# A state-space scan cut into two spans of chunks, with the router of the mixture inside the second span

## The chip, the cores and the metric

The kernel runs on one core of a Trainium2 chip. The metric is the time of one execution on the device, in microseconds, lower is better. The time before is 2651.47 us, the median of three runs (2647.59 to 2654.21). The profile is of one execution on the same core, with a span of 2646.7 us.

The program drives five engines, each with its own list of instructions: TensorE (PE in the rows; its weight loads are PEld), VectorE (DVE), ScalarE (ACT), GpSimd (POOL) and SyncE (SP, which only issues DMAs here).

## The reference, cut to what matters

Two layers work on 4096 tokens (two sequences of 2048) of width 256. The first layer (attention and a fused mixture, up to about 1607 us in the profile) is not touched. The second has a state-space block and a mixture of 20 experts of which each token takes two, each followed by a residual and a layer norm:

```python
# state-space block: u is (2, 2048, 256), 16 states per channel
A = -jnp.exp(log_A)
dt = jax.nn.softplus(u @ W_dt.T + b_dt + dt_bias)
Bt = (u @ W_B.T + b_B).reshape(b, l, d, n)
Ct = (u @ W_C.T + b_C).reshape(b, l, d, n)
A_bar = jnp.exp(dt[..., None] * A)
x_in = (A_bar - 1.0) / A * Bt * u[..., None]
# h = A_bar * h + x_in along the tokens; y = sum over n of Ct * h; y + D_skip * u
x = _layernorm(x + y)

# mixture of experts: E = 20, K = 2
h = gelu(xf @ wg1 + bg1)
probs = softmax((h @ wg2 + bg2)[:, :E])
top_vals, top_idx = top_k(probs, 2)
y = sum over the two chosen experts of top_val * (xf @ We[e] + be[e])
x = _layernorm(x + y)
```

## The kernel before

The tokens are cut into 8 chunks of 512 (CH); a chunk is 4 tiles of 128 tokens. The 256 channels are two halves (KT) of 128 partitions.

**The scan** (`phase_scan`, L1618). The work is 256 units: for each of the 16 states n, for each half m of the channels, for each of the 8 chunks. TensorE (L1681 to L1703) makes B and C of the unit, each from six products in fp32r (high and low parts of weights and tokens, L1684 to L1686), into rings of four and two PSUM banks. ScalarE makes the decay exp(dt A) (`decay`, L1724) and copies C with its scale (`outward`, L1732). VectorE makes (B + b) u (`driven`, L1838), times (decay - 1) (`decayed`, L1845), and the recurrence over 512 tokens (`scan`, L1853, instruction L1858). GpSimd multiplies the states by C (`multiply`, L1791, instruction L1797) and adds them to y (L1812). Each pair (n, m) needs its own weights; they are loaded raw, copied by ScalarE into the high part, and VectorE takes the low part from the two (`round_w`, L1826, instruction L1831), once for 8 units. The low parts of the tokens are made at the start (`round_lo`, L1833, instruction L1835, and L1816 on GpSimd). The states of n = 1 to 14 are a loop in each engine's program.

**The mixture** (`phase_mixture`, L1958) is a block of its own that begins when all engines have left the scan. First, for each chunk, comes what is called gating below. `turn_z` (L2133) turns y by 8 transposes, ScalarE copies it, VectorE takes mean and variance (`means`, L2406) and normalises (`normalise`, L2416). `turn_x` (L2143) turns it back by 8 transposes, `hide` (L2151) is the hidden layer, ScalarE applies gelu, `logits` (L2162) gives the 20 scores. The tiles form three groups of 8, 12 and 12 (chunks 0 and 1; 2 to 4; 5 to 7). For each group VectorE takes softmax and the two largest (`choose`, L2429), TensorE counts how many tokens chose each expert (`count`, L2172), VectorE turns the counts into a place for each token in a list sorted by expert (`settle`, L2454, and `list_tiles`, L2473), and GpSimd writes the tokens' rows to their places in DRAM by indirect DMAs (`scatter`, L2103, instruction L2108: 16, 24 and 24 of them).

Then 62 pairs of list tiles (18, 22 and 22 for the groups) go through the experts: SP loads a pair's 256 rows (`load`, L2075), TensorE turns them (`turn_rows`, L2184, instruction L2191), ScalarE copies them, TensorE multiplies them by the expert's weights and adds the bias (`experts`, L2194, instructions L2202 and L2203), ScalarE (first 18 pairs) or VectorE copies the answer, and SP stores it. The gating of chunks 5 to 7 lies among the first pairs (`hide(5)` at pair 3, `count(2)` at pair 14, `exponent(2)` on ScalarE at pair 11). GpSimd gathers the answers back by 64 indirect DMAs (`gather`, L2111, instruction L2119), those of the last group only when all pairs are stored; VectorE combines (`combine`, L2487) and normalises (`finish`, L2504), and ScalarE's queue stores the output.

## Time and profile before

| | |
|---|---|
| median of three runs | 2651.47 us |
| the profiled execution: its span | 2646.7 us |
| TensorE busy | 93% of the span |
| VectorE, ScalarE, GpSimd busy | 74%, 52%, 42% |
| mean granted TensorE clock | 0.972 |
| first matmul of the scan | 1610.0 us |
| end of the scan on TensorE | about 2340.2 us |
| first expert product | 2415.0 us |
| last expert product | about 2601.2 us |

The profiled execution has no time of its own beside its span; the difference of 4.8 us to the median is the part outside the first and the last instruction, and the spread of the runs. All positions are from the span's start. A row of stretches names for each engine its busy time in the stretch and in brackets how many instructions; matmuls are pipelined, so that two of them overlap in the rows and a mean duration is longer than the time from one start to the next.

### The profile page before, as it was taken

The numbers are of one execution on the slowest core, as the hardware profiler recorded it, in microseconds if no ns is written. First come the engines' busy times: TensorE is split into PE (matmuls) and PEld (weight loads), VectorE is DVE, ScalarE is ACT, GpSimd is POOL, SyncE is SP. The second block draws the span as 40 slices with busy tenths as digits, with TensorE's granted clock in tenths as the row PEclk, the third lists the DMA queues.
The fourth block names the chain that finished last, engine by engine and source line by source line (L and its number), as shares of the span: only waits on it lengthen the run. The fifth ranks groups of instructions, "written<-read, shape, count | busy, mean of one in ns | idle before, by whom it ended". The sixth has DMA issues, their size and how long they took to land. (4 is left out here: it accounts for less than half of the span.)

```text
span 2646.7 us, 43896 instructions
## 1 busy us (share of the span) xinstructions
PE 2472.2 (93%) x15059; PEld 1552.6 (59%) x15059; DVE 1964.7 (74%) x4037; ACT 1382.1 (52%) x2469; POOL 1110.7 (42%) x1092
## 2 busy tenths in 40 slices
PE   7999999999999999899999997999999999977992
PEld 4433333333333333467777775888888888855772
DVE  3777777777777774266676657999999999975256
ACT  3466666666666666444455535655555555543320
POOL 3522222222222221110000004999989898944454
PEclk9999999999999999999999998999999999987996
DMA  8633333323333321100000000000000000024785
GB/s 244 174 70 71 82 58 58 58 58 58 58 58 69 70 64 66 54 16 17 16 24 25 9 17 8 13 12 12 12 12 12 12 12 12 4 86 130 238 282 162
DMA packets 109601, 166.41 MB, mean 63 GB/s; under 512 B 15876, under 2 KB 74296, under 8 KB 106232
## 3 DMA queue, kind: packets, MB, share of 16 engines
q1 hardware_dynamic: 99064, 143.24, 21.5%
q0 software_dynamic: 6144, 16.79, 2.0%
q10 hardware_dynamic: 4224, 4.19, 0.5%
q8 instruction: 99, 1.62, 0.3%
q14 instruction: 70, 0.57, 0.1%
HBM read 97.66 MB, written 62.01 MB: 60 GB/s over the span
## 5 line engine op out<-in xcount | busy, mean ns | idle before, releaser
L644 ACT ACTIVATE ssm_in_dt<-att_s 128x512 f32<-128x512 f32 (+3 forms) x1280 | 610.0, 535 | 346.9 <-PE att_s L541 182.7
L733 DVE TENSOR_REDUCE att_partmax<-att_s 128x1 f32<-128x512 f32 x768 | 494.3, 686 | 109.8 <-PE att_s L515 66.4
L541 PE MATMUL att_s<-att_qs,att_ks 49*128 49x512 f32 (+3 forms) x1280 | 433.9, 419 | 16.1 <-ACT ssm_in_dt L644 13.8
L515 PE MATMUL att_s<-att_ks,att_qs 49*128 49x512 f32 (+3 forms) x1280 | 434.5, 424 | 4.9 <-DVE att_qs L723 4.7
L541 PEld LDWEIGHTS att_s<-att_qs,att_ks 49*128 49x128 f32 x1280 | 207.4, 185 | 380.3 <-ACT ssm_in_dt L644 307.6
L1797 POOL TENSOR_TENSOR ssm_cc<-ssm_cc,ssm_h 128x512 f32<-128x512 f32 x256 | 334.9, 1308 | 75.7 <-DVE ssm_h L1858 73.8
L432 POOL TENSOR_SCALAR_AFFINE_SELECT ssm_in_dt<-ssm_in_dt 128x256 f32<-128x256 f32 x256 | 104.6, 409 | 621.5 <-ACT ssm_in_dt L644 562.8
L584 PE MATMUL att_o_ps<-ssm_in_dt,att_vst 128*32 128x512 f32 (+3 forms) x2560 | 340.6, 542 | 5.3 <-ACT ssm_in_dt L644 5.3
L1812 POOL TENSOR_TENSOR ssm_out_z<-ssm_out_z,ssm_cc 128x512 f32<-128x512 f32 x256 | 340.4, 1330 | 0.1
L1737 ACT ACTIVATE ssm_cc<-ssm_c_ps,ssm_cur 128x512 f32<-128x512 f32 x256 | 199.0, 777 | 211.8 <-PE ssm_c_ps L1686 211.5
L736 DVE CUSTOM_DVE_ANT_0 att_hid<-att_s,att_hidden 128x512 bf16<-128x512 f32 (+3 forms) x512 | 238.8, 487 | 94.6 <-PE att_s L515 93.7
L1858 DVE TENSOR_TENSOR_SCAN ssm_h<-ssm_a_ps,ssm_h,ssm_inp 128x512 f32<-128x512 f32 x192 | 243.8, 1270 | 0.1
L1730 ACT ACTIVATE ssm_a_ps<-ssm_in_dt,ssm_cur 128x512 f32<-128x512 f32 x256 | 176.4, 689 | 114.5 <-DVE ssm_h L1858 108.5
L515 PEld LDWEIGHTS att_s<-att_ks,att_qs 49*128 49x128 f32 x1280 | 203.9, 185 | 28.1 <-DVE att_partmax L733 10.8
L1842 DVE SCALAR_TENSOR_TENSOR ssm_inp<-ssm_b_ps,ssm_cur,ssm_in_u 128x512 f32<-128x512 f32 x256 | 190.0, 742 | 34.5 <-PE ssm_b_ps L1686 32.7
L1684 PE MATMUL ssm_b_ps<-ssm_hi,ssm_w_hi 128*128 128x512 f32 x512 | 203.5, 398 | 12.7 <-DVE ssm_lo L1835 11.2
L1684 PE MATMUL ssm_c_ps<-ssm_hi,ssm_w_hi 128*128 128x512 f32 x512 | 203.2, 397 | 0.0
L1685 PE MATMUL ssm_c_ps<-ssm_lo,ssm_w_hi 128*128 128x512 f32 x512 | 203.2, 397 | 0.0
L1686 PE MATMUL ssm_c_ps<-ssm_hi,ssm_w_lo 128*128 128x512 f32 x512 | 202.9, 396 | 0.0
L1686 PE MATMUL ssm_b_ps<-ssm_hi,ssm_w_lo 128*128 128x512 f32 x512 | 202.8, 396 | 0.0
L1685 PE MATMUL ssm_b_ps<-ssm_lo,ssm_w_hi 128*128 128x512 f32 x512 | 202.4, 395 | 0.0
L1850 DVE SCALAR_TENSOR_TENSOR ssm_inp<-ssm_a_ps,ssm_inp 128x512 f32<-128x512 f32 x256 | 169.2, 661 | 0.0
(324 smaller groups left out, 4183.7 us busy)
## 6 DMA issues: line engine op xcount, KB each, us to landing
qk_halves<-ssm_in_dt SPq DMA_DIRECT2D x64, 256.0 KB
moe_sorted<-att_hidden SPq DMA_DIRECT2D x31, 512.0 KB, 9.4
moe_rows<-moe_sorted SPq DMA_DIRECT2D x62, 256.0 KB
moe_answers<-moe_mixed SPq DMA_DIRECT2D x62, 256.0 KB
att_far<-bias_tables SPq DMA_DIRECT2D x96, 136.0 KB, 8.5
att_stage_q<-qk_halves SPq DMA_DIRECT2D x96, 128.0 KB, 4.4
att_stage_k<-qk_halves SPq DMA_DIRECT2D x96, 128.0 KB, 5.9
ssm_raw<-in_w_bc SPq DMA_DIRECT2D x30, 256.0 KB, 2.6
```

What stands on the lines that cost most here:

```text
L515: mm = nc.tensor.matmul(s1[:, S1_BANK[at], 0:hi - lo], qs[p % 3][half(b, ROWS), I * P:(I + 1) * P], ks[p % 3][half(b, ROWS), lo:hi], start ...
L541: mm = nc.tensor.matmul(s2[:, turn % RING, 0:hi - lo], ks[p % 3][half(b, ROWS), J * P:(J + 1) * P], qs[p % 3][half(b, ROWS), lo:hi], start ...
L584: mm = nc.tensor.matmul(o_ps[32 * g:32 * g + 32, b, lo:CH], vst[p % 2][b][:, J, :], prob[:, b, step % 2, x * CH + lo:(x + 1) * CH], start= ...
L644: nc.scalar.activation(prob[:, b, step % 2, x * CH + lo:(x + 1) * CH], s2[:, turn % RING, 0:CH - lo], ACT.Exp, scale=1.0 / HD).then_inc(s2 ...
L733: nc.vector.tensor_reduce(most, piece, AX, ALU.max).then_inc(s1_read, 1)
L736: nc.vector.tensor_tensor_reduce(out=hid[HID[at]][:, 0:width], in0=piece, in1=hidden[:, CH - width:CH], scale=1.0, scalar=-3.0e38, op0=ALU ...
L1684: nc.tensor.matmul(out, w_hi, hi[:, k, tok], start=first, stop=False)
L1685: nc.tensor.matmul(out, w_hi, lo[:, k, tok], start=False, stop=False)
L1686: return nc.tensor.matmul(out, w_lo, hi[:, k, tok], start=False, stop=last)
L1797: nc.gpsimd.tensor_tensor(at, at, h[:, i % H_RING], ALU.mult).then_inc(multiplied, 1)
L1812: nc.gpsimd.tensor_tensor(part, part, cc[:, i % Y_RING], ALU.add).then_inc(y_added, 1)
L1858: nc.vector.tensor_tensor_scan(h[:, i % H_RING], a_ps[:, i % A_RING], inp[:, i % 2], 0.0 if first else h[:, (i - 1) % H_RING, CH - 1:CH], ...
```

## The change

The scan and the mixture become one block with one list of instructions for each engine, written out without loops.

- The 256 units are gone through in two parts: first chunks 0 to 4 for all 32 pairs (n, m) (160 units), then chunks 5 to 7 (96 units). The last state of chunk 4 of each pair is kept (`keep_state`) and begins chunk 5. The low and high weights of each pair are stored to DRAM in the first part (512 KB each) and loaded again in the second (`store_halves`, `load_halves`).
- Between the units of the second part stands the gating of chunks 0 to 4, the choices of groups 0 and 1, and the 16 scatters of group 0, at fixed units (`gate(c)` is 161 + 7c). The expert weights are loaded there too, over the parts of u and dt that are no longer read. The 24 scatters of group 1 follow on GpSimd directly behind the last unit.
- The gating of chunks 5 to 7 stands among the pairs, with `turn_z` too (`gate_pair(c)` is 3(c - 5)); `count(2)` moves from pair 14 to 18, `exponent(2)` from 11 to 17. ScalarE copies the answers of 20 pairs instead of 18.
- B has two PSUM banks instead of four, the decay three instead of two; one bank (`spare`) serves all steps of the gating. `round_w` reads the raw weights from this bank, where ScalarE copies them, instead of from SBUF.
- y lies in two segments of 256 tokens for each chunk, so that its transposition can be written over it; GpSimd's addition writes two segments.
- On chunks 0 to 4 ScalarE normalises, and copies both halves of the turned rows.
- A pair's list tiles are interleaved: partition p takes rows 2p and 2p + 1 of the pair (2 KB in one piece) where it took rows p and p + 128 (twice 1 KB). The places that the scatters and gathers use follow it (five small VectorE instructions more for each group).

The diff's core, in the order SyncE, TensorE (units, then pairs), GpSimd, VectorE. `turn_z(c, s)` waits until GpSimd has done the addition of the chunk's last unit (`y_added`).

```diff
-        A_RING, B_RING, C_RING = 2, 4, 2
-        H_RING, Y_RING = 4, 8
+        A_RING, B_RING, C_RING, H_RING, Y_RING = 3, 2, 2, 4, 8
+PART_CHUNKS = ((0, 1, 2, 3, 4), (5, 6, 7))
+HELD = len(PART_CHUNKS[0])
+SPLIT = BLOCKS * HELD
+def gate(turn):
+    return SPLIT + 1 + 7 * turn
+def gate_pair(c):
+    return 3 * (c - HELD)
...
+            def load_halves(b):
+                if b < KT:
+                    eng.wait_ge(halves_stored[b], 16 * N)
+                    eng.wait_ge(c_ready, SPLIT - (KT - 1 - b) * HELD)
+                else:
+                    eng.wait_ge(c_ready, first_unit(b - 1, 1))
+                eng.dma_start(halves[b % KT][:].rearrange("p a k c -> p (a k c)").bitcast(F32), t.halves_bc[b]).then_inc(halves_loaded[b % KT], 16)
...
-                eng.dma_start(rows[p % ROWS][:], t.rows[h][2 * n * P:2 * (n + 1) * P, :].rearrange("(j p) d -> p j d", p=P)).then_inc(rows_loaded[p % ROWS], 16)
+                eng.dma_start(rows[p % ROWS], t.rows[h][2 * n * P:2 * (n + 1) * P, :].rearrange("(p j) d -> p j d", j=2)).then_inc(rows_loaded[p % ROWS], 16)
...
+            for g in range(UNITS):
+                states(g)
+                for c in range(HELD):
+                    for s in range(2):
+                        if g == gate(c) + s:
+                            turn_z(c, s)
+                    for k in range(KT):
+                        if g == gate(c + 2) + 2 + k:
+                            turn_x(c, k)
+                    if g == gate(c + 2) + 4:
+                        hide(c)
+                    if g == gate(c + 3) + 6:
+                        logits(c)
+                if g == gate(6) + 5:
+                    count(0)
+                if g == gate(9) + 5:
+                    count(1)
             turn_rows(0)
             turn_rows(1)
...
             for p in range(PAIRS_ALL):
+                for c in range(HELD, NCH):
+                    for s in range(2):
+                        if p == gate_pair(c) + s:
+                            turn_z(c, s)
+                    if p == gate_pair(c) + 5:
+                        turn_x(c, 0)
+                        turn_x(c, 1)
+                    if p == gate_pair(c) + 6:
+                        hide(c)
+                    if p == gate_pair(c) + 8:
+                        logits(c)
-                if p == 14:
+                if p == 18:
                     count(2)
...
+            for g in range(UNITS):
+                if g + 1 < UNITS:
+                    multiply(g + 1)
+                add(g)
+                for n in range(GROUP_TILES[0]):
+                    for k in range(2):
+                        if g == gate(7) + 3 + 4 * n + 2 * k:
+                            scatter(0, n, k)
+            for n in range(GROUP_TILES[1]):
+                for k in range(2):
+                    scatter(1, n, k)
...
+            for g in range(UNITS):
+                scan(g)
+                if g + 1 < UNITS:
+                    decayed(g + 1)
...
+                if g + 2 < UNITS:
+                    driven(g + 2)
...
+                if g == gate(8) + 2:
+                    share(1)
+                for q in range(3):
+                    if g == gate(8) + 3 + q:
+                        largest(1, q)
+                    if g == gate(8) + 6 + q:
+                        whose(1, q)
+                if g == gate(9) + 2:
+                    chosen(1)
+                if g == gate(9) + 3:
+                    joined(1)
+                if g == gate(9) + 4:
+                    spots(1)
+                if g == gate(9) + 5:
+                    places(1)
```

## Rows read from the trace of the kernel before

**Rows 1.** Busy time by stretch: scan's start, scan, gating, pairs, tail.
```profile
core 0: us, PE busy (x) PEld busy (x) DVE busy (x) ACT busy (x) POOL busy (x), PEclk, DMA share, GB/s
1610.00:1700.00 90.00, 82.16 (x331) 64.03 (x332) 86.80 (x99) 62.08 (x92) 72.33 (x52) 0.96 0.04 12
1700.00:2340.00 640.00, 639.83 (x2743) 513.63 (x2741) 607.71 (x714) 338.70 (x512) 577.85 (x458) 1.00 0.04 11
2340.00:2414.00 74.00, 41.60 (x193) 29.82 (x194) 48.45 (x203) 29.24 (x46) 23.24 (x24) 0.72 0.37 127
2414.00:2471.00 57.00, 50.81 (x276) 39.63 (x275) 18.79 (x82) 22.88 (x39) 23.14 (x24) 0.92 0.56 176
2471.00:2601.00 130.00, 119.90 (x664) 96.80 (x662) 66.05 (x151) 30.72 (x55) 61.41 (x64) 0.97 0.82 262
2601.00:2647.00 46.00, 0.24 (x2) 0.00 (x0) 25.96 (x76) 1.19 (x4) 22.83 (x24) 0.53 0.42 129
```
**Rows 2.** TensorE's waits between 1595 and 1720 us: in total, times, longest.
```profile
PE ssm_b_ps L1684 <- DVE ssm_lo L1835: 11.2, 4, 4.9
```
**Rows 3.** VectorE: one unit of the scan in order of time, and `round_w`, grouped and alone.
```profile
1903.59 1.27 DVE L1858 TENSOR_TENSOR_SCAN ssm_h<-ssm_a_ps,ssm_h,ssm_inp 128x512 f32<-128x512 f32 x1
1905.36 0.73 DVE L1842 SCALAR_TENSOR_TENSOR ssm_inp<-ssm_b_ps,ssm_cur,ssm_in_u 128x512 f32<-128x512 f32 x1
1906.02 1.27 DVE L1858 TENSOR_TENSOR_SCAN ssm_h<-ssm_a_ps,ssm_h,ssm_inp 128x512 f32<-128x512 f32 x1
...
L1831 DVE TENSOR_TENSOR ssm_w_lo<-ssm_raw,ssm_w_hi 128x512 fp32r<-128x512 f32 x27 | 45.4, 1683 | 0.0
```
**Rows 4.** GpSimd in order of time at the scan's end.
```profile
2337.83 1.30 POOL L1797 TENSOR_TENSOR ssm_cc<-ssm_cc,ssm_h 128x512 f32<-128x512 f32 x1 [0.30 <-DVE ssm_h L1858]
2339.09 1.27 POOL L1812 TENSOR_TENSOR ssm_out_z<-ssm_out_z,ssm_cc 128x512 f32<-128x512 f32 x1
2344.28 2.67 POOL L1812 TENSOR_TENSOR ssm_out_z<-ssm_out_z,ssm_cc 128x512 f32<-128x512 f32 x2
```
**Rows 5.** TensorE in order of time: the gating's four steps, and turns of pairs.
```profile
2367.78 1.10 PE L2140 MATMUL moe_z_ps<-moe_ident,ssm_out_z 128*128 128x128 f32 x8
2425.54 1.04 PE L2148 MATMUL moe_xT_ps<-moe_ident,moe_x 128*128 128x128 f32 x8
2426.41 0.60 PE L2191 MATMUL moe_z_ps<-moe_ident,moe_rows 128*128 128x128 f32 x4
2445.07 1.06 PE L2169 MATMUL moe_lg_ps<-moe_g,moe_hT 64*128 64x20 f32 x8
2446.06 1.98 PE L2159 MATMUL moe_rt_ps<-moe_xT,moe_g 128*128 128x512 f32 x4
2447.88 0.60 PE L2191 MATMUL moe_z_ps<-moe_ident,moe_rows 128*128 128x128 f32 x4
2491.49 0.60 PE L2191 MATMUL moe_z_ps<-moe_ident,moe_rows 128*128 128x128 f32 x4
2493.88 0.60 PE L2191 MATMUL moe_z_ps<-moe_ident,moe_rows 128*128 128x128 f32 x4
```
**Rows 6.** Group 2's choice: table load before its exponent, TensorE's count, VectorE's last step.
```profile
2460.26 1.28 ACT L2296 ACT_TABLE_LOAD   x1
2469.93 0.28 PE L2178 MATMUL moe_rt_ps<-moe_both,moe_earlier 128*128 128x260 bf16 x1 [4.03 <-DVE moe_both L2452]
2470.76 0.85 PE L2191 MATMUL moe_z_ps<-moe_ident,moe_rows 128*128 128x128 f32 x4
2476.42 0.19 DVE L2479 TENSOR_SCALAR moe_cols<-moe_expert 128x44 int32<-128x44 f32 x1
```
**Rows 7.** GpSimd's scatters: all (ns min/median/max), and two in order of time.
```profile
L2108 POOL DMA_INDIRECT moe_sorted<-moe_x,moe_place x64: 957/963/1466, 2381.7 to 2517.6; - x64
...
2383.41 0.97 POOL L2108 DMA_INDIRECT moe_sorted<-moe_x,moe_place  x1 [0.30 <-issue]
2384.68 0.96 POOL L2108 DMA_INDIRECT moe_sorted<-moe_x,moe_place  x1 [0.30 <-issue]
```
**Rows 8.** DMA issues by size: KB each, median us from issue to landing.
```profile
moe_w<-in_we SPq DMA_DIRECT2D x10, 512.0 KB, 7.8
ssm_raw<-in_w_bc SPq DMA_DIRECT2D x30, 256.0 KB, 2.6
```
**Rows 9.** SP's DMA queue: 2490 to 2520 us (pairs), then 2350 to 2370 us (expert weights).
```profile
q1 hardware_dynamic: 6754, 6.52, 71.0%
...
q1 hardware_dynamic: 3584, 5.46, 79.1%
```

More of the change, by code:

```diff
@@ new lines, in phase_scan @@
+        hi, lo = sp.sb("hi", [P, HELD, KT, CH], F32R), sp.sb("lo", [P, HELD, KT, CH], F32R)
+        halves = [sp.sb(f"halves{m}", [P, 2, KT, 2 * P], F32R) for m in range(KT)]
+        raw_sb = sp.sb("raw", [P, KT, KT * 2 * P])
+        inp = sp.sb("inp", [P, 2, CH])
+        h = sp.sb("h", [P, H_RING, CH])
+        cc = sp.sb("cc", [P, Y_RING, CH])
+        par = sp.sb("par", [P, 5, KT, N])
+        skip = sp.sb("skip", [P, KT])
+        carry = sp.sb("carry", [P, BLOCKS])
+        one = sp.sb("one", [P, 1])
@@ new lines, in phase_scan @@
+        pick = mx.sb("pick", [EB, 3])
+        be_pad = mx.sb("be_pad", [P, E2 * D], BF16)
+        three = mx.sb("three", [P, P], BF16)
+        earlier, all_ones = mx.sb("earlier", [P, P], BF16), mx.sb("all_ones", [P, P], BF16)
+        ones20 = mx.sb("ones20", [P, E2])
+        hTs = mx.sb("hT", [P, 2, CH])
+        pr = [mx.sb(f"pr{s}", [P, MAXT, E2]) for s in range(2)]
+        red, inv = mx.sb("red", [P, MAXT]), mx.sb("inv", [P, MAXT])
+        top = mx.sb("top", [P, NT, 8])
+        topi, topf = mx.sb("topi", [P, MAXT, 8], U32), mx.sb("topf", [P, MAXT, 2])
@@ new lines, in phase_scan @@
+        mine = mx.sb("mine", [P, 2, MAXT, E2])
+        both = mx.sb("both", [P, MAXT + 1, E2], BF16)
+        number, rounds = mx.sb("number", [P, E2], I32), mx.sb("rounds", [P, E2])
+        upto, before = mx.sb("upto", [P, E2]), mx.sb("before", [P, E2])
+        work = mx.sb("work", [P, MAXL * E2])
+        place_f = mx.sb("place_f", [P, 2, MAXT])
+        place_i, within, odd = (mx.sb("place_i", [P, 2, MAXT], I32), mx.sb("within", [P, 2, MAXT], I32), mx.sb("odd", [P, 2, MAXT], I32))
+        place = [mx.sb(f"place{h}", [P, 2, GROUP_TILES[h]], U32) for h in range(NG3)]
@@ new lines, in phase_scan @@
+        expert = mx.sb("expert", [P, MAXL])
+        cols = [mx.sb(f"cols{h}", [P, GROUP_LIST[h]], I32) for h in range(NG3)]
+        stats, mv = mx.sb("stats", [P, TPC, 6]), mx.sb("mv", [P, NT, 2])
+        std, rstd, less = mx.sb("std", [P, NT]), mx.sb("rstd", [P, NT]), mx.sb("less", [P, NT])
+        stats2, mv2 = mx.sb("stats2", [P, 2, TPC, 6]), mx.sb("mv2", [P, 2, TPC, 2])
+        std2, rstd2 = mx.sb("std2", [P, 2, TPC]), mx.sb("rstd2", [P, 2, TPC])
+        raw = raw_sb[:].rearrange("p m (k c) -> p m k c", k=KT)
@@ new lines, in hT_of, with turned_bank, hidden_bank, along @@
+        def hT_of(c):
+            return hTs[0:HG, c % 2] if c < HELD else h[0:HG, c % 2]
+        def turned_bank(c, k):
+            return spare if c < HELD else a_ps[:, k]
+        def hidden_bank(c):
+            return spare if c < HELD else a_ps[:, 2]
+        def along(x, tiles):
+            return x.unsqueeze(1).to_broadcast([P, tiles, E2])
+        def over(x, tiles):
+            return x.unsqueeze(2).to_broadcast([P, tiles, E2])
+        def spot_of(tiles):
+            return work[:, 0:tiles * E2].rearrange("p (n e) -> p n e", e=E2)
@@ L2479, in list_tiles @@
+                step(nc.vector.tensor_reduce(expert[:, 0:length], passed, AX, ALU.add))
                 nc.vector.tensor_scalar(cols[h][:], expert[:, 0:length], float(E2 - 1), float(D), ALU.min, ALU.mult).then_inc(cols_ready, 1)
@@ L2545, in _ @@
+            whole_normalise(7)
             read_x(7)
-            choose(2)
-            settle(2)
+            read_logits(6)
+            read_logits(7)
+            shift(2)
+            share(2)
+            for q in range(3):
+                largest(2, q)
+            for q in range(3):
+                whose(2, q)
+            chosen(2)
+            joined(2)
+            spots(2)
+            places(2)
+            passes(2)
             list_tiles(2)
```

1236 lines of the change are left out of this document (634 added, 602 removed).

## The prediction

> **What bounds the kernel now.** I read the page first, for the shares and slices, then cut the part behind 1610 us into stretches [rows 1]. The scan is bound by TensorE: between 1700 and 2340 us it is busy without a gap, 2743 matmuls in 640 us, 0.2333 us each, so a unit of 12 takes 2.80 us. VectorE follows closely, 607.7 of 640. Behind the scan come 74 us in which TensorE is busy for 41.6 at a granted clock of 0.72, a mean of stretches at 1.2 and 2.4 GHz: the block's start, and gating in which each engine waits for another. The pairs then run 187 us, and a tail of 45.5 us follows in which TensorE does nothing and the last 24 gathers, combinations and stores set the end. Only the 74 us are idle enough to be worth moving; the 640 before them have no TensorE time to give away, so what is moved there costs its own TensorE time.
>
> The order of time gives the rates. VectorE repeats a unit of the scan in 1906.02 - 1903.59 = 2.43 us when nothing holds it, leaving 0.37 us in 2.80 [rows 3]. GpSimd's multiply and add start 1.26 us apart, 2.52 a unit, leaving 0.28 [rows 4]. A pair of experts takes TensorE 2493.88 - 2491.49 = 2.39 us [rows 5].
>
> **The change, part by part, against the span of 2646.7 us.**
>
> *The 74 us go.* The first expert product no longer stands behind the gating of chunks 0 to 4: -74.
>
> *Gating inside the scan.* At full clock, start to start [rows 5]: turning back 2426.41 - 2425.54 = 0.87, scores 0.99, hidden layer 2447.88 - 2446.06 = 1.82 or a little more (I take 1.9), and the turn of y like the other eight transposes, 0.87 (1.10 at most). That is 4.63 a chunk, 23.2 for five; the two counts take 2470.76 - 2469.93 = 0.83 each [rows 6]. Sum +24.8. Nothing hides it, since TensorE is full.
>
> *The scan itself.* 256 units of 2.80 stay. At its start TensorE waits 11.2 us for low parts of the tokens [rows 2]; in 1610 to 1700 it issues 331 matmuls where 386 would fit, 13 us lost. Three of the eight roundings move to unit 155 and later. They spare perhaps 4 us at the start, and there fall on VectorE at up to 2 us each with 0.37 a unit to spare, about 3 us. I take 0 for both, bounds -5 to +5. `round_w` costs 1.68 us with both inputs in SBUF [rows 3]; it is done 32 times, with one input from PSUM, at something between the 0.73 of `driven` and 1.68. VectorE has room for either, so the term is 0.
>
> *Fewer B banks.* TensorE may write B of unit g+2 when `driven(g)` has read B of g. B takes half a unit, so it comes back 1.4 us before B of g+2 is complete at 5.6: `driven` may be late by 5.6 - 1.4 - 0.73 = 3.4 us. C has had two banks all along and allows 5.6 - 1.4 - 0.8 = 3.4 too. Cost 0 as long as VectorE lags by less.
>
> *VectorE beside it.* While gating stands on TensorE too, a unit has more room. The choice of group 1 does not have that: between units 216 and 233 it wants, by group 2's as it ran, about 13 us (2461.6 to 2469.9 and 2470.9 to 2476.6 less its waits, and five small instructions of 0.2) [rows 6]; these 17 units have 17 x 0.37 = 6.3 us, and 3.4 may be late. About 4 us reach TensorE; with small ones elsewhere +5, bounds 0 and 20.
>
> *Scatters on GpSimd.* One is issued each 1.27 us [rows 7]. Sixteen in 32 units: 16 x 1.27 = 20.3, room 32 x 0.28 = 9, so GpSimd ends 11 us behind and gets back 3 by the last unit. Eight buffers of C and four of h carry most of it, but at the first pair `turn_z(5)` waits until the additions of chunk 5 are done. Without a lag that is about 3 us behind the last matmul, as the last additions end at 2346.95 against TensorE's 2340.2 [rows 4]. With 8 us of lag it is 11, of which the two turns of rows cover 1. I take +8, bounds 3 and 14. If GpSimd keeps up, this term is where I am too high.
>
> The Trainium skill, "SBUF — State Buffer", section "SBUF: two separate sides", says that a DMA issued by GpSimd can't write its descriptors while VectorE holds the port that both share, and gives 3100 ns for one that takes 620 alone. By that each of the 16 would cost 2 us more, 34 in all. The scan's VectorE instructions read one input from PSUM, which that section doesn't count among the holders. Here the longest of 64 took 1.47 us beside VectorE's normalisation [rows 7].
>
> *Weights out and in.* 32 stores and 32 loads of 512 KB, where raw loads of 256 KB land in 2.6 us and ten of 512 KB at once in 7.8 [rows 8]. `load_halves` is issued a block of three units, 8.4 us, before its use, longer where gating lies between. Both ends are below that: 0. If this cover were gone by 1 us a block it would cost 32.
>
> *Pairs.* Work: 62 x 2.39 = 148.2, three chunks of gating 13.9, a count 0.8: 163. Waits: at `turn_x(5)` and `turn_x(6)` the statistics of the following chunk stand first on VectorE, 1 us each: 2. `count(2)` now comes 1 pair behind `exponent(2)`. From the table load to the count were 9.7 us [rows 6], less 2.4 of a pair: a stall of 7.5, where it was 4. Behind the count, 48 pairs took 130 us for 114.7 of work [rows 1], 15 lost, mostly in the last 50 us, where loads and stores fill the queues. There the rows' layout helps: with pieces of 1 KB the queue moved 6.52 MB in 71% of 30 us, 306 GB/s while busy; the expert weights, 2 KB in one piece, 5.46 MB in 79.1% of 20 us, 345 [rows 9]. I let 8 of the 15 stay (bounds 3 and 15). Sum 163 + 2 + 7.5 + 8 = 180.5, against 187: -6.5.
>
> *Tail.* 24 gathers at GpSimd's pace in both: 0.
>
> Sum: -74 + 24.8 + 0 + 5 + 8 - 6.5 = -42.7. From the span that is 2604; with the 4.8 us between the span and the median, **2609 us**.
>
> **Rivals.**
>
> A. *The inserts disturb the scan* (0.18). VectorE's and GpSimd's room is 10 to 13% of a unit. ScalarE's table changes, 1.28 us each way [rows 6], and chains of waits come on top, and every program is in order. If the 96 units run at 3.1 instead of 2.8: +29, 2638. For it: DVE at 95% [rows 1]. Against: the inserts bring TensorE work with them, which stretches the unit for all.
>
> B. *The pairs run clean* (0.15). Pieces of 2 KB take the DMA waits away and GpSimd keeps up: 3 instead of 8, a start of 3 instead of 8, and the count's stall at 4: -13, 2596.
>
> C. *GpSimd becomes the bound, slower* (0.07). Its addition now writes two segments of 256. No row has that; the nearest is the contiguous addition, 1.26. Up to 1.54 the scan holds its pace; from 1.70 (39 us over 256 units on top of the 0.28) the whole gain is gone. At 1.9 a unit takes 3.16: +92, 2700.
>
> D. *Scatters wait for VectorE* (0.04). Each waits for a scan instruction of 1.27 to end: 16 x 1.27 = 20 more, 2629. By the skill's figure it would be 34.
>
> E. *The reloads are late* (0.04): 1.2 us a block, 38 us, about 2648: the change does not what it says, the time goes from one stage into the other.
>
> **How the numbers follow.** The forecast has 0.52. A measurement of this kernel tells 0.3%, 8 us, from no change: same is 2643.5 to 2659.4. Faster: 0.52 + 0.15 + 0.15 of A + 0.03 of D = 0.85. Same: 0.03 of A, 0.01 of D, 0.02 of E = 0.06. Slower: C and 0.02 of E = 0.09. The forecast's own bounds (scan ±5, VectorE 0 to 20, GpSimd 3 to 14, pairs 3 to 15) give 2590 to 2630 when not all fall on one side. The range takes in B and most of A: 2585 to 2645.
>
> **What the profile would show.** One stretch without a gap from the scan into the pairs, at full clock; between units 161 and 233 a unit pace of 3.1 to 3.3 us where gating stands, 2.8 elsewhere; the first expert product near 2340 + 25 + 5 + 9 = 2379; there a wait of `turn_z` on GpSimd's addition; a wait for `both` before the third count; the last expert product near 2559; a tail of 45. Wrong would be: `scan`'s add on GpSimd over 1.5 us; TensorE waiting for `halves` at each block; a pace above 2.8 in the first 160 units; pairs at over 2.6 us in the last 40.

## The result

The changed kernel takes 2665.3 us (five runs, 2664.2 to 2667.5) where the kernel before takes 2651.3 (2647.6 to 2654.2): 1.0062 times as long by the ratio on record, 95% interval 1.005 to 1.0074 (the two medians alone give 1.0053). The forecast was 2609, faster. It was wrong in its sign: 43 us less were expected of the span, 19 more came (2646.7 to 2665.7).

The profile after, by stretches, to be held against [rows 1]. The columns are the same; the first part of the scan ends at 2058, the scan at 2382, the pairs at 2620.

```profile
core 0: us, PE busy (x) PEld busy (x) DVE busy (x) ACT busy (x) POOL busy (x), PEclk, DMA share, GB/s
1610.00:1700.00 90.00, 84.28 (x350) 67.72 (x351) 84.63 (x106) 62.73 (x97) 73.16 (x54) 0.95 0.17 60
1700.00:2040.00 340.00, 340.00 (x1502) 281.64 (x1501) 325.35 (x408) 205.59 (x326) 316.11 (x252) 1.00 0.17 58
2058.00:2382.00 324.00, 296.52 (x1306) 236.15 (x1305) 288.51 (x467) 189.40 (x271) 256.95 (x205) 0.97 0.23 77
2382.00:2394.00 12.00, 3.67 (x21) 3.24 (x20) 3.55 (x6) 2.60 (x5) 12.00 (x10) 0.71 0.14 44
2394.00:2620.00 226.00, 178.26 (x949) 142.75 (x947) 85.30 (x243) 63.65 (x107) 85.90 (x90) 0.88 0.59 196
2620.00:2666.00 46.00, 0.00 (x0) 0.00 (x0) 25.04 (x74) 1.19 (x4) 22.79 (x24) 0.53 0.41 126
```

Three things stand in it. The first part of the scan is faster than before: 1502 matmuls in 340 us, 0.2264 us each, where [rows 1] has 0.2333. The second part has 27 us in which TensorE stands. And the pairs take 226 us, where the forecast had 180.5 and the kernel before 187; TensorE works for 178 of them.

What TensorE waits for between 2058 and 2394 (who, for whom; us in total, times, longest); the kernel before has no wait at all there until 2340:

```profile
PE ssm_ps L1963 <- ACT ssm_out_z L2151: 10.9, 5, 2.8
PE ssm_ps L1963 <- POOL ssm_out_z L2307: 8.3, 1, 8.3
PE ssm_ps L1939 <- DVE ssm_inp L2369: 6.7, 5, 2.7
PE ssm_ps L2017 <- DVE moe_both L2525: 6.6, 1, 6.6
PE ssm_ps L1978 <- ACT ssm_raw L2172: 1.8, 2, 1.5
PE ssm_ps L2004 <- DVE moe_work L2538: 1.4, 1, 1.4
```

The second line is the wait of the first pair for the last additions of chunk 5, forecast at 8. The others add up to 27.4 us inside the scan, forecast at 5. With 96 units of 12 x 0.2264 (260.8) and 24.8 of gating that is 313; TensorE is busy 11 longer than this work wants at full clock, if gating costs the 24.8 of the forecast. The granted clock is 0.88 between 2300 and 2350, a mix of 1.2 and 2.4 GHz, behind the 6.6 us before the second count. 313 + 11 = 324, the length of the stretch. The mean clock of 0.97 over the 324 us can cost some 10 us at most (324 x 0.03); it is most of the 11, and was not measured apart from gating.

VectorE in the choice of group 1, in order of time (start, us):

```profile
2262.69 2.85 DVE L2493 TENSOR_TENSOR moe_pr<-moe_pr,moe_red 128x240 f32<-128x240 f32 x1
...
2295.59 2.84 DVE L2518 CAST moe_topf<-moe_topi 128x24 f32<-128x24 uint32 x1
...
2311.72 1.97 DVE L2544 TENSOR_TENSOR moe_work<-moe_mine,moe_work 128x240 f32<-128x240 f32 x2
...
2322.54 3.82 DVE L2558 TENSOR_TENSOR moe_work<-moe_order_f,moe_upto 128x880 f32<-128x880 f32 x1
```

2.84 us for a conversion of 24 elements a partition cannot be its work: another one of 24 elements (L2548) takes 0.18 here. These instructions read only the state buffer, as `round_w` did in [rows 3] (1.68 us), and GpSimd has an operation in hand all the time here.

In the pairs, TensorE's three longest stalls with one turn of y between them, and what ScalarE does at that time ("remote" is a wait that ended with the raising of a semaphore, but at a moment at which no instruction's record on this core ends that could have raised it):

```profile
2391.75 1.09 PE L1963 MATMUL ssm_ps<-moe_ident,ssm_out_z 128*128 128x128 f32 x4 [8.33 <-POOL ssm_out_z L2307]
...
2402.53 0.60 PE L1963 MATMUL ssm_ps<-moe_ident,ssm_out_z 128*128 128x128 f32 x4
...
2413.38 1.11 PE L1963 MATMUL ssm_ps<-moe_ident,ssm_out_z 128*128 128x128 f32 x4 [7.87 <-issue]
...
2433.73 1.94 PE L1978 MATMUL ssm_ps<-moe_ident,ssm_out_z 128*128 128x128 f32 x8 [15.17 <-DVE ssm_out_z L2473]
```

```profile
2407.82 0.58 ACT L2200 COPY ssm_cc<-ssm_ps 128x512 f32<-128x512 f32 x1 [4.43 <-remote]
...
2412.74 0.58 ACT L2151 COPY ssm_out_z<-ssm_ps 128x512 f32<-128x512 f32 x1 [2.73 <-remote]
...
2417.73 0.58 ACT L2193 COPY ssm_cc<-ssm_ps 128x512 f32<-128x512 f32 x1 [4.40 <-remote]
2429.68 0.58 ACT L2200 COPY ssm_cc<-ssm_ps 128x512 f32<-128x512 f32 x1 [11.37 <-remote]
```

Take the copy at 2412.74. It waits for the turn of y that TensorE's record has at 2402.53 to 2403.13. The trace also holds the moments at which semaphores are raised, which the rows above don't print, and there this turn's semaphore is raised only at 2412.72; ScalarE starts 0.02 us later. The four semaphores of TensorE that end ScalarE's first four such waits are raised at 2402.78, 2407.79, 2412.72 and 2417.70, 5 us apart, and four more together between 2429.66 and 2429.89, while TensorE's own records go on at their usual pace as long as it has work. So what is late is the raising of TensorE's semaphores; ScalarE does not dawdle. VectorE has such waits too (5 of the 15 behind 2340 us), and every one of the 15 ends less than 7 us behind at least two indirect DMAs (scatters or gathers) that GpSimd issued. Why the semaphores are late no run shows.

GpSimd issues the 24 scatters of group 1 back to back at that time, from 2395.62 to 2425.7, 1.27 us apart as in [rows 7]. The diff takes away their waits for turned rows; I had read that edit and given it no term. The third count waits 6.2 us, as forecast (7.5, in place of 4.03 in [rows 6]):

```profile
2489.09 0.37 PE L2017 MATMUL ssm_ps<-moe_both,moe_earlier 128*128 128x260 bf16 x1 [6.21 <-DVE moe_both L2525]
```

Stores and loads of the weights' halves land far below a block's 8.4 us (last column: median us to landing), so rival E is out; and GpSimd's addition in two segments costs what its multiplication does (mean ns ahead of the second bar), so C is out too.

```profile
scan_halves<-ssm_halves SPq DMA_DIRECT2D x32, 512.0 KB, 2.9
ssm_halves<-scan_halves SPq DMA_DIRECT2D x32, 512.0 KB, 3.4
```

```profile
L2307 POOL TENSOR_TENSOR ssm_out_z<-ssm_out_z,ssm_cc 128x512 f32<-128x512 f32 x81 | 105.7, 1305 | 0.0
L2298 POOL TENSOR_TENSOR ssm_cc<-ssm_cc,ssm_h 128x512 f32<-128x512 f32 x81 | 104.5, 1290 | 56.3 <-DVE ssm_h L2393 49.1 <-ACT ssm_cc L2129 6.9
```

### The profile page after: what moved, and what is told of

Same layout as the page of the kernel before. It is cut to its first block and busy times, and to the rows that moved or that the text cites. A ratio compares the mean times of both kernels' runs of the same rounds, so it can differ in the third digit from the quotient of the medians.

```text
span 2665.7 us, 43081 instructions
## 1 busy us (share of the span) xinstructions
PE 2460.0 (92%) x15059; PEld 1555.8 (58%) x15059; DVE 1938.6 (73%) x4031; ACT 1432.2 (54%) x2544; POOL 1111.3 (42%) x1092
## 3 DMA queue, kind: packets, MB, share of 16 engines
q1 hardware_dynamic: 91128, 176.80, 24.8%
## 5 line engine op out<-in xcount | busy, mean ns | idle before, releaser
L644 ACT ACTIVATE ssm_in_dt<-att_s 128x512 f32<-128x512 f32 (+3 forms) x1280 | 609.9, 535 | 347.6 <-PE att_s L541 182.9
L1939 PE MATMUL ssm_ps<-ssm_hi,ssm_halves 128*128 128x512 f32 x1024 | 409.5, 400 | 16.0 <-DVE ssm_lo L2364 7.1
L1940 PE MATMUL ssm_ps<-ssm_lo,ssm_halves 128*128 128x512 f32 x1024 | 403.3, 394 | 0.0
L1941 PE MATMUL ssm_ps<-ssm_hi,ssm_halves 128*128 128x512 f32 x1024 | 402.9, 393 | 0.0
L2129 ACT ACTIVATE ssm_cc<-ssm_ps,ssm_par 128x512 f32<-128x512 f32 x256 | 198.4, 775 | 162.7 <-PE ssm_ps L1941 162.6
L2123 ACT ACTIVATE ssm_ps<-ssm_in_dt,ssm_par 128x512 f32<-128x512 f32 x256 | 177.0, 692 | 140.4 <-DVE ssm_h L2393 138.6
L1939 PEld LDWEIGHTS ssm_ps<-ssm_hi,ssm_halves 128*128 128x128 f32 x1024 | 194.9, 190 | 62.7 <-DVE ssm_inp L2369 9.1
L2369 DVE SCALAR_TENSOR_TENSOR ssm_inp<-ssm_ps,ssm_par,ssm_in_u 128x512 f32<-128x512 f32 x256 | 190.8, 745 | 51.2 <-PE ssm_ps L1941 49.9
L1941 PEld LDWEIGHTS ssm_ps<-ssm_hi,ssm_halves 128*128 128x128 f32 x1024 | 194.8, 190 | 41.5
L1940 PEld LDWEIGHTS ssm_ps<-ssm_lo,ssm_halves 128*128 128x128 f32 x1024 | 194.9, 190 | 40.4 <-issue 1.2
L2393 DVE TENSOR_TENSOR_SCAN ssm_h<-ssm_ps,ssm_h,ssm_inp 128x512 f32<-128x512 f32 x160 | 203.6, 1272 | 0.6
L2375 DVE SCALAR_TENSOR_TENSOR ssm_inp<-ssm_ps,ssm_inp 128x512 f32<-128x512 f32 x256 | 170.3, 665 | 0.0
```

Of the source, the lines that this page charges most:

```text
L644: nc.scalar.activation(prob[:, b, step % 2, x * CH + lo:(x + 1) * CH], s2[:, turn % RING, 0:CH - lo], ACT.Exp, scale=1.0 / HD).then_inc(s2 ...
L1939: nc.tensor.matmul(out_ps, halves[m][:, 0, k, col], hi[:, slot, k], start=k == 0, stop=False)
L1940: nc.tensor.matmul(out_ps, halves[m][:, 0, k, col], lo[:, slot, k], start=False, stop=False)
L1941: mm = nc.tensor.matmul(out_ps, halves[m][:, 1, k, col], hi[:, slot, k], start=False, stop=k == KT - 1)
L2393: nc.vector.tensor_tensor_scan(h[:, g % H_RING], a_ps[:, g % A_RING], inp[:, g % 2], begin, ALU.mult, ALU.add).then_inc(h_ready, 1)
```

## The experiments

They ran in six sets, each beside the kernel before. The sets are of two kinds, and one chip was met in both. In sets 1 to 3 ScalarE has no "remote" wait behind 2340 us and the kernel before takes 2631 to 2633 us; in sets 4 to 6, as in the first measurement, it has 18 to 47 us of them and the kernel before takes 2645 to 2652. "Standstills" below are these waits for late semaphores. So times and traces are compared within a set, and ratios to the kernel before within a kind. The table has, from the profiled runs, the end of the last product of the scan, the start of the first pair's bias product, the end of the last pair's, and the span. The scan begins between 1605.5 and 1618.6 us in these executions, so that two ends of a scan can lie some us apart without a difference in the scan; where it matters, the text takes this off.

| run | set | scan's end | first | last | span | pairs | ratio to before, 95% |
|---|---|---|---|---|---|---|---|
| before, first | - | 2339.8 | 2416.6 | 2601.2 | 2646.7 | 184.7 | |
| after, first | - | 2382.5 | 2395.2 | 2619.6 | 2665.7 | 224.4 | 1.0062 (1.005 to 1.0074) |
| e1_gated | 1 | 2380.8 | 2393.5 | 2579.0 | 2624.1 | 185.5 | 0.9977 (0.9967 to 0.9986) |
| e3_before_pe_flat | 1 | 2338.2 | 2411.3 | 2581.5 | 2626.8 | 170.2 | 0.9993 (0.9983 to 1.0003) |
| e4_no_adds | 1 | 2365.2 | 2376.8 | 2564.0 | 2609.1 | 187.2 | 0.9948 (0.9931 to 0.9965) |
| e5_copies_first | 1 | 2372.4 | 2384.9 | 2570.8 | 2615.7 | 185.9 | 0.9941 (0.9925 to 0.9958) |
| r_before | 2 | 2335.3 | 2408.8 | 2579.7 | 2624.7 | 170.9 | |
| r_after | 2 | 2381.0 | 2393.7 | 2577.7 | 2622.7 | 184.0 | 0.9974 (0.9958 to 0.999) |
| e7_all | 2 | 2364.9 | 2367.7 | 2547.9 | 2592.9 | 180.3 | 0.9866 (0.9849 to 0.9883) |
| e8_no_scatter0 | 2 | 2376.2 | 2381.6 | 2565.5 | 2610.5 | 183.9 | 0.9931 (0.9914 to 0.9947) |
| e6_gated_old_layout | 3 | 2377.3 | 2390.1 | 2573.1 | 2618.1 | 182.9 | 0.9968 (0.9958 to 0.9978) |
| e9_tokens_as_before | 3 | 2380.9 | 2393.8 | 2576.0 | 2621.1 | 182.2 | one run |
| e10_before_two_b | 3 | 2337.4 | 2410.4 | 2579.9 | 2625.1 | 169.5 | one run |
| after_again | 4 | 2376.7 | 2389.2 | 2609.8 | 2656.1 | 220.6 | 1.005 (1.0031 to 1.0068) |
| e17_best | 4 | 2362.2 | 2365.0 | 2568.7 | 2614.0 | 203.7 | 0.9883 (0.9864 to 0.9903) |
| e14_before_banks | 4 | 2341.4 | 2418.0 | 2603.1 | 2648.7 | 185.1 | one run |
| e16_small_last | 4 | 2318.8 | 2394.4 | 2578.3 | 2623.8 | 184.0 | one run |
| spread_again | 5 | 2389.4 | 2402.1 | 2600.0 | 2644.9 | 197.9 | 0.9973 (0.9962 to 0.9985) |
| e20_after_shifted | 5 | 2396.9 | 2408.1 | 2628.6 | 2673.5 | 220.6 | 1.0114 (1.0097 to 1.0132) |
| e19_weights_first | 6 | 2319.4 | 2394.9 | 2578.5 | 2624.8 | 183.6 | one run |

### Scatters in one go, or spread

```diff
 for n in range(GROUP_TILES[1]):
     for k in range(2):
+        after(eng, rowsT_ready, 4 + 12 * (2 * n + k) // (2 * GROUP_TILES[1]))
         scatter(1, n, k)
```

> The changed kernel with one edit: the 24 scatters of group 1, issued in one go behind the scan, wait for the turned rows of pairs 4 to 15, as they did before. Theory (the burst): while GpSimd issues 24 scatters 1.27 us apart (2395.6 to 2425.7), ScalarE stands four times without a semaphore's reason (4.4, 2.7, 4.4, 11.4 us) and TensorE twice (7.9 and 15.2). Spread over the pairs, both stalls go, but for what single scatters cost: 18 to 22 us less, 2645 +- 5; TensorE busy over 42 of 50 us in 2400 to 2450, not 25. Rival (the stall belongs to the start of the pairs: first code, first rows, the rows' way through memory): it stays where it is whatever the scatters do, 2665 +- 4. Second rival: the spread scatters cost each pair as much in all as the burst did; then no single stall is left but the pairs stay at 225 us, 2665.

0.9977 of the kernel before. The changed kernel itself, in the next set, came to 0.9974, so that the edit was worth nothing there:

> The changed kernel as it is, once more. In the last set of runs the kernel before took 2630.8 us where it had taken 2651.3, and a version that still issues the 24 scatters in one go showed TensorE busy for 42.6 of 50 us in 2400 to 2450, where the changed kernel had 25.3. Theory (the stall behind the burst of scatters, 23 us of TensorE, comes with the chip or what runs beside it): here the changed kernel takes 2628 +- 4, as fast as before, and the window shows over 40 of 50. Rival (the burst always stalls it, and the other version escaped by its timing): 2645 or more, the window under 30.

> The kernel before as it is, for its trace beside the others of this set. If the 20 us between the two sets lie in the scatters and pairs, its scan ends at 2340 +- 5 as before and the 8.4 us in which ScalarE and VectorE stood at 2396.7 are gone; if the whole chip is faster, the scan ends 10 or more earlier.

The kernel before is 20 us faster in this set; its scan ends at 2335.3, 4.5 earlier, but also begins 4.5 earlier (1605.5, not 1610.0), and its pairs take 170.9 in place of 184.7. The standstills are absent in both kernels, so these runs cannot tell whether the burst of scatters matters where they occur.

> The changed kernel as it is. If what it lost first (224 us in the pairs) belongs to some chips, it comes out either near 2665 with the kernel before near 2651, or near 2624 with the kernel before near 2632, and nothing between. If it comes with single executions whatever the chip, some of these rounds are 20 us and more above the others.

1.005 again, pairs of 220.6 us. No round stands out (2654.6 to 2665.0): the standstills come with a set, not with single executions. They don't come with the chip, as this expectation and others have it: the chip of sets 2 and 3 had them in set 6. ScalarE's waits in this run between 2394 and 2600:

```profile
ACT ssm_cc L2193 <- PE ssm_ps L2030: 60.2, 23, 8.0
ACT ssm_cc L2193 <- remote: 20.2, 4, 7.3
ACT ssm_cc L2200 <- remote: 16.6, 2, 12.8
```

The wait of 12.8 us ends at 2420.2, half a microsecond behind the last scatter (2418.78 + 0.96).

> The changed kernel with group 1's scatters spread over pairs 4 to 15. If the kernel before takes near 2650 here (a chip on which the changed kernel took 1.005 of it and ScalarE stood 12.8 us behind the burst): theory (burst) 15 to 23 us less than that, 0.997 to 0.999 of the kernel before, pairs 200 to 205 us; rival (the stall belongs to the start of the pairs) 1.004 or more, pairs over 215. If the kernel before takes near 2631: 0.9977 +- 0.001 again, and it tells nothing new.

A set of that kind: 0.9973, against 1.005 for the changed kernel in set 4. (This profiled execution, 2646.7 us, is the slowest of its twelve, and its scan begins latest of all, at 1618.6; their median is 2637.0.) ScalarE's "remote" waits fall from 39.8 us to 18.4, the longest from 12.8 to 5.9, and the pairs from 220.6 to 197.9:

```profile
ACT ssm_cc L2193 <- remote: 14.7, 3, 5.9
...
ACT ssm_cc L2200 <- remote: 3.7, 1, 3.7
```

The same set has a version that issues them in one go, e20_after_shifted below: its pairs take 220.6. It is shown that issuing 24 scatters in one go costs some 20 us where the standstills occur and nothing where they don't. Why TensorE's semaphores are raised late, and what makes a set of one kind, stays open. The kernel before has such waits too (20.8 us at its copies of rows, 2.9 at its copy of answers), each of them likewise behind indirect DMAs of GpSimd; I had read them as DMA waits.

### What GpSimd does to VectorE

```diff
+if gate(7) + 6 <= g + 2 <= gate(10) + 4:
+    eng.sem_inc(y_added, 1)
+    return
 nc.gpsimd.tensor_tensor(part, part, cc[:, g % Y_RING]..., ALU.add).then_inc(y_added, 1)
```

> The changed kernel without GpSimd's additions into y in the units in which group 1 is chosen (22 of 256; that part of the output is left out; its semaphore is still raised). Theory (the port): small VectorE instructions with two inputs in the state buffer wait for the GpSimd operation that runs (2.85 us for one of 0.38 alone, 2.84 for a cast of 24 elements). With half of GpSimd's work gone they get shorter, to between half and a fifth; the wait before the second count falls from 6.6 us to under 3, TensorE's short waits for VectorE's input of a unit (0.6 to 2.7, four of them) go: 8 to 12 us less, 2655 +- 3. Rival (the load): VectorE is late by the sum of its own work; the small ones keep 2.5 to 2.8 us each and the time falls by under 3 us.

The same four instructions of VectorE without the additions beside them, in order of time:

```profile
2257.14 0.41 DVE L2496 TENSOR_TENSOR moe_pr<-moe_pr,moe_red 128x240 f32<-128x240 f32 x1
...
2285.55 0.33 DVE L2521 CAST moe_topf<-moe_topi 128x24 f32<-128x24 uint32 x1
...
2298.57 0.87 DVE L2547 TENSOR_TENSOR moe_work<-moe_mine,moe_work 128x240 f32<-128x240 f32 x2
...
2308.29 1.21 DVE L2561 TENSOR_TENSOR moe_work<-moe_order_f,moe_upto 128x880 f32<-128x880 f32 x1
```

2.85 becomes 0.41, 2.84 becomes 0.33, 3.82 becomes 1.21. TensorE's waits for VectorE's input fall from 6.7 to 1.3 us and the one before the count from 6.6 to 4.0. The scan ends at 2365.2, 15.6 us earlier than in e1_gated, whose scan is the changed kernel's, of which 2.4 are an earlier beginning. Part of it is the clock: between 2260 and 2350 it is 0.98, where e1_gated has 0.92. This profiled execution is the fastest of its four; by the medians of the set (2616.3 against 2625.5) the edit is worth 9 us, within the 8 to 12 expected. The load theory is out: VectorE is late because its longest instructions here stand behind a GpSimd operation. Many of the small ones keep their lengths (the 0.18 of L2548). The Trainium skill, "SBUF — State Buffer", section "SBUF: two separate sides", says just that: a VectorE instruction with two inputs in the state buffer, or in its mode with two ports, and a GpSimd operation that reads the state buffer shut each other out for a whole instruction. The trace agrees for two inputs (2.85 against 0.41), and the one with an input from PSUM keeps its 0.41 (L2538, 128 x 240). The conversion has one input; in which mode it runs no row shows, nor why L2548 is spared.

### The order on ScalarE

```diff
-if g + 1 < UNITS:
-    decay(g + 1)
 for c in range(HELD):
     ...  copy_z, copy_x, gelu
+if g + 1 < UNITS:
+    decay(g + 1)
 outward(g)
```

> The changed kernel with one edit: in the second part of the scan ScalarE copies turned y and x and does the hidden layer ahead of the next unit's exponential, not behind it. Theory (order on ScalarE): TensorE waits for the copy of the first half of a chunk before it turns the second (2.78, 1.79, 2.70, 1.79, 1.79) and twice for a copy of x (0.3, 1.5), as the copy stands behind an exponential that waits for VectorE's scan. In front of it the waits shrink to under 0.5 each: 8 to 10 us less, 2656 +- 3. Rival (VectorE bounds these units): the exponential is then late, VectorE's instructions of the next unit with it, and TensorE waits for VectorE in place of ScalarE: within 3 us of 2665.

0.9941, or 8.6 us under e1_gated by the medians; the scan ends at 2372.4, 8.4 us earlier than there (it begins 3.1 later), and TensorE waits 3.1 us for copies, not 10.9. For VectorE's input it waits 7.9, not 6.8, so little comes back. The theory holds; the rival doesn't.

### Scatters in the scan

```diff
 if g == gate(7) + 3 + 4 * n + 2 * k:
-    scatter(0, n, k)
+    eng.sem_inc(scattered[0], 16)
```

> The changed kernel without the 16 scatters of group 0 in the scan (its sorted rows are then not written, and its pairs compute on what the memory holds; the semaphore is raised 16 times in their place). Theory of the prediction (scatters make GpSimd late): GpSimd's last addition ends 3 us behind TensorE's last product of the scan, not 9; the wait at the first turn of chunk 5 is 3 instead of 8.3; 5 to 6 us less than the changed kernel. Rival (GpSimd is late by its additions in two segments, 1.31 us, and by VectorE's lateness): the wait stays at 6 or more and the time within 3 us.

The wait at the first pair falls from 8.4 to 2.6 us as the prediction's theory says. The whole is 10 us, not 6: TensorE's waits for VectorE fall too (input 6.7 to 3.6, second count 6.6 to 5.1).

### The layout of rows

```diff
-step(nc.vector.tensor_copy(listed, place_f[:, :, 0:tiles]))
-...  rest, second, place_f
-nc.vector.tensor_tensor(place[h][:], place_f[:, :, 0:tiles], rest, ALU.add).then_inc(place_ready, 1)
+nc.vector.tensor_copy(place[h][:], place_f[:, :, 0:tiles]).then_inc(place_ready, 1)
-... .rearrange("(p j) d -> p j d", j=2)
+... .rearrange("(j p) d -> p j d", p=P)
```

> The changed kernel with group 1's scatters spread over the pairs and the rows of a pair laid out as before (two pieces of 1 KB a partition; the four small VectorE instructions that turn a place into its new position are gone). Theory of the prediction (pieces of 2 KB take some 7 us of DMA waits from the last pairs): with 1 KB pieces the pairs, 185.5 us with the new layout, take 190 to 195 and the kernel 5 to 10 us longer than the same with 2 KB pieces (0.9977 of the kernel before), so 1.000 to 1.0015. Rival (the pairs of the kernel before take 171 us in these runs with pieces of 1 KB; the layout is worth nothing): 0.9977 +- 0.001, pairs 185 +- 2.

0.9968, pairs 182.9: in a set without standstills pieces of 1 KB are as good as pieces of 2 KB, and the old layout spares four small VectorE instructions in each group (five go, a copy takes their place). TensorE waits 8.3 us for rows here and 7.0 in e1_gated. The prediction's 7 us are refuted for such sets; with standstills the two layouts were not compared.

### Where the faster products come from

```diff
-with eng.Fori(0, N) as n:                                  # e3, in the kernel before
+for n in range(N):
-hi, lo = sp.sb("hi", [P, HELD, KT, CH], F32R), ...         # e9, in the changed kernel
+hi, lo = (sp.sb(x, [P, KT, HELD * CH], F32R)[:].rearrange(...) for x in ("hi", "lo"))
-A_RING, B_RING, C_RING = 2, 4, 2                           # e10 and e14, in the kernel before
+A_RING, B_RING, C_RING = 2, 2, 2
+a_ps, b_ps, c_ps = ps[:, 0:2], ps[:, 3:5], ps[:, 5:7]      # e14 alone, and w_hi, w_lo in one tensor
```

> The kernel before with one edit: TensorE's program of the scan is written out for all 16 states, where it was a loop over the states with the body once. The other engines keep their loops. The changed kernel has it written out, and takes 0.2265 us from the start of one matmul to the next in its first part, where the kernel before took 0.2333. Theory (the loop): the 3 per cent belong to the way TensorE fetches its program; here the scan runs at 2.72 us a unit instead of 2.80, up to 256 x 0.08 = 20 us less, 2631 to 2640. Rival (operands): they belong to the new places of tokens, weights or banks; here nothing changes, 2651 +- 3, 0.233 us a matmul. Second rival: a program written out has to be fetched and is slower, 2655 or more.

> The changed kernel with the rounded tokens in the order of before: half of the channels of all chunks, then the other half, instead of chunk by chunk. It looks for the cause of 0.2265 us from matmul to matmul where the kernel before has 0.2333. If the place of the moving operand sets it, 0.233 here in 1700 to 2000 us (x429 of 100 us); if not, 0.2265 (x443).

> The kernel before with two banks for B instead of four, as the changed kernel has. If the number of banks that products rotate through sets the pace, x443 matmuls in 100 us and a scan that ends 15 to 20 us earlier; if not, x430. If two banks hold TensorE up, as the prediction's bound of 3.4 us says they don't, waits of TensorE for VectorE's first instruction of a unit appear.

> The kernel before with the banks where the changed kernel has them (A in 0 and 1, B in 3 and 4, C in 5 and 6) and each weight's two halves in one tensor. If one of these places sets 0.2333 us a matmul, x443 in 100 us; if not, x430.

Four misses. TensorE's program written out, the order of tokens, the number of banks and their places with the halves in one tensor change nothing: 430 matmuls in 100 us where it was 430 (1287 in 300 with two banks and with the banks moved), and 1326 in 300 in the changed kernel with the old order of tokens.

```diff
-skip, par, cur = ...          # 8 + 640 + 40 bytes a partition
 raw = sp.sb("raw", [P, 2, KT, 2 * P])
 w_hi, w_lo, inp, h, cc = ...
+skip, par, cur = ...
```

> The kernel before with its three small parameter tensors (688 bytes a partition) behind the large ones in the state buffer, so that weights, input, states and products start at round addresses as in the changed kernel. Theory (an operand at an odd place slows matmuls or what runs beside them): x443 in 100 us and a scan that ends 15 to 20 us earlier. Rival (places don't matter): x430.

That was it. The view by stretches, in this version of the kernel before:

```profile
1700.00:2000.00 300.00, 300.00 (x1325) 248.49 (x1324) 293.51 (x348) 165.66 (x249) 280.80 (x223) 1.00 0.04 12
```

Its scan ends at 2318.8, 22.6 us earlier than that of e14_before_banks in the same set (it begins 3.0 earlier), and its one run took 2625.5 us beside 2647.2. The reverse, in the changed kernel:

```diff
+par, skip, pad = ...          # 688 bytes a partition
 halves = [sp.sb(f"halves{m}", [P, 2, KT, 2 * P], F32R) for m in range(KT)]
```

> The changed kernel with 688 bytes of small tensors between the rounded tokens and the weights, so that weights, raw weights, input, states and products stand where they are not at round addresses, as in the kernel before. Theory (places): x430 matmuls in 100 us, a scan 2 to 3 per cent longer (12 to 20 us), and the time as much over that of the changed kernel. Rival (the new tensors' own shapes give the pace): x443, within 3 us of the changed kernel.

```profile
1700.00:2000.00 300.00, 300.00 (x1287) 240.98 (x1287) 280.79 (x351) 175.50 (x278) 272.18 (x215) 1.00 0.17 58
```

The pace of before, and 1.0114 instead of 1.005. The last run (set 6) has the small tensors of the kernel before between the weights and the rest:

> The kernel before with its 688 bytes of small tensors between the weights (raw and rounded) and the input, states and products. If the place of the weights, which TensorE loads, gives the pace: x443 matmuls in 100 us between 1700 and 2000, as with the small tensors behind all. If the place of what VectorE, ScalarE and GpSimd use gives it: x430. A number between says that both do.

```profile
1700.00:2000.00 300.00, 300.00 (x1325) 248.43 (x1324) 292.15 (x347) 165.46 (x250) 278.84 (x221) 1.00 0.04 12
```

So it is the place of the weights. The raw and the rounded ones moved together in these edits; TensorE reads the rounded ones alone. One run, 2626.6 us beside 2652.0. Which steps of the address matter wasn't tried.

### The edits together

```diff
+ scatters spread; ScalarE's copies first (both as above)
-count(1) at gate(9) + 5, spots(1) at gate(9) + 4, places(1) at gate(9) + 5, lists at gate(10) + 1
+count(1) at gate(9) + 7, spots(1) at gate(9) + 6, places(1) at gate(9) + 7, lists behind the scan
-gate_pair(c) = 3 * (c - HELD);  exponent(2) at 17, count(2) at 18;  BY_SCALAR = 20
+gate_pair(c) = 3 * (c - HELD) + 2;  exponent(2) at 19, count(2) at 22;  BY_SCALAR = 24
-group 2's scatters wait for pairs 19 + 15 * (2 * n + k) // 24
+group 2's scatters wait for pairs 22 + 13 * (2 * n + k) // 24
```

> The changed kernel with these edits at once: group 1's scatters wait for turned rows of pairs 4 to 15; ScalarE's copies of gating go ahead of the next exponential; the second count comes two units later and group 1's list of tiles is made behind the scan; the first chunk of the last three is turned two pairs later (pairs 0 and 1 run before GpSimd has added the last y); the last count comes at pair 22, not 18, and ScalarE copies the answers of 24 pairs, not 20. Theory (the losses are single waits of known length): it spares 9 at ScalarE's copies, 5 to 9 at VectorE in the choice, 6 at the first pair, 8 to 12 at the last count: 28 to 36 less than the changed kernel beside it, 2597 +- 6. Rival (VectorE and GpSimd are the bound of the second part, and what is spared at one wait comes back at the next): 10 to 15 less, 2615 +- 4.

0.9866, 27 us under the changed kernel of its set, a little less than the theory's 28 to 36 and far from the rival's 10 to 15. The longest of what TensorE still waits for between 2368 and 2550:

```profile
PE ssm_ps L2030 <- DMA ssm_raw<-moe_sorted: 3.5, 4, 1.6
PE ssm_ps L2030 <- DMA ssm_inp<-moe_sorted: 3.4, 1, 3.4
PE ssm_ps L1963 <- POOL ssm_out_z L2307: 2.3, 1, 2.3
PE ssm_ps L2017 <- DVE moe_both L2526: 1.4, 1, 1.4
```

> The version with all the single edits (copies first, scatters spread, later counts, first chunk of the last three two pairs later) and besides with the rows of a pair laid out as before. With the spread scatters alone the old layout spared 3.5 us in the scan and 2.6 in the pairs. Theory (two groups' four small VectorE instructions in a full scan cost TensorE time): 3 to 6 us under the version without it, 0.985 of the kernel before +- 0.001. Rival (their time is hidden now that the counts come later): 0.9866 +- 0.001.

0.9883 in a set with standstills, where the changed kernel has 1.005: it beats both kernels there, by 31 and 43 us. Whether the old layout adds to it can't be told, as the version without it ran in a set of the other kind.

## Why the prediction was wrong

The forecast's steps against the first measurement, in us of the span:

| step | forecast | measured | difference |
|---|---|---|---|
| place of the weights: 3072 x (0.2333 - 0.2264) | 0 | -21.2 | -21.2 |
| TensorE's waits in the scan's second part | +5 | +27.4 | +22.4 |
| gating's TensorE time and the clock in that part, together | +24.8 | +35.7 | +10.9 |
| from the scan's end to the first expert product | 9 | 11 | +2 |
| pairs | 180.5 | 226.1 | +45.6 |
| tail | 45.5 | 46.1 | +0.6 |

The differences add up to 60.3; from -42.7 to +19.0 it is 61.7. The rest is mostly the scan's beginning, 1.7 us later than before (1611.7 against 1610.0).

*The 74 us went* as said: from the scan's last product to the first bias product it is 12.6 us, not 76.7. *Gating's own time* at 24.8 is not contradicted: the 10.9 over it are about what the granted clock can have cost.

*VectorE beside the scan* is the first failed step. I counted the instructions of group 2's choice at the lengths that they had while GpSimd did no arithmetic (four scatters, 3.85 us busy in 2461.6 to 2476.6), 13 us, and gave the total a room of 9.7. Beside GpSimd's additions the four rows above alone last 11.5 us where e4_no_adds has 2.8. With these 8.7 more the 5 would have been about 14; TensorE waited 14.7 us for VectorE (6.7 + 6.6 + 1.4), and 6.7 without the additions. A hint was at hand: `round_w` at 1.68 us in [rows 3]. (With one input from PSUM it now takes 0.67 to 0.68, a little under the bounds given.) I applied the port rule to the scatters, where it did nothing much (mean 1073 ns, against 963), and not to the choice.

*ScalarE's order* had no term, only a mention under rival A. Its 10.9 us are A's chain of waits: copy behind exponential, exponential behind VectorE's scan. A's mechanism was right and its price (29) close to the 22 + 11; the first pace of 2.72 us hid it in the time of the scan.

*The first pair* waits 8.33 us for GpSimd, forecast 8, and for the reason given: without the scatters of group 0 it is 2.6. *The count* waits 6.2 us, forecast 7.5.

*The pairs* are the second failed step, and the larger one. "8 of the 15 stay" rested on a false cause: the 15 us lost in the kernel before's pairs are mostly the standstills, waits for late semaphores of TensorE (pairs 184.7 with them, 170.9 without), not queues full of 1 KB pieces, and the layout moves none. The diff also takes the waits from 24 scatters, and the forecast gave this nothing: of the 39.7 us by which the pairs grew in the first measurement, 22.7 go when the scatters are spread (220.6 to 197.9). The other 13 are there in both kinds of set (184.0 against 170.9; 197.9 against 184.7). They are mostly TensorE's own time and the third count. In the pairs of r_before, then of r_after:

```profile
2407.30:2579.70 172.40, 163.39 (x931) 131.79 (x929) 84.78 (x230) 53.98 (x94) 84.55 (x88) 0.99 0.81 256
...
2392.00:2577.70 185.70, 168.11 (x950) 135.42 (x949) 85.60 (x244) 63.60 (x107) 86.88 (x90) 0.97 0.72 238
```

TensorE is busy 4.7 us longer, and it waits 6.2 us for the count, not 1.0. In sets without standstills the pairs take 184.0, near the forecast; but the kernel before has 170.9 there, so that the step's change (-6.5) fails in both kinds, by 20 and by 46.

*An effect nobody asked for* works the other way. The new order of tensors puts the weights at another place and makes each product 3 per cent shorter. With the small tensors ahead of the weights the changed kernel takes 1.0114. The regrouping as such costs 1 per cent, and the place of the weights gives about half of it back; the kernel before with that one move (0.992 in set 4, one run) is faster than the changed kernel.

## What to carry to other kernels

Before moving small work beside a busy stage, take its durations from a stretch in which the same neighbours run, and look for each instruction at whether its inputs are in the state buffer or in PSUM. Put the waits of a taken-away throttle into the sum as carefully as those of an added one. And when a diff rearranges tensors, look at the pace of one unchanged inner instruction before explaining anything else.
